# A gated delta-rule mixer: the last query-key projection of a chunk pair goes ahead of the fourth value projection

## What is computed

```python
q, k, v = x @ w_q, x @ w_k, x @ w_v
beta = sigmoid(x @ w_b) * 2.0
g = -exp(A_log) * softplus(x @ w_a + dt_bias)
q, k, v = [silu(causal_conv4(t, w)) for t, w in ((q, conv_q), (k, conv_k), (v, conv_v))]
q, k = l2norm(q), l2norm(k)                      # per head
for t in range(2048):                            # state S, 64 x 128 for each head
    S = S * exp(g[t])
    delta = (v[t] - k[t] @ S) * beta[t]
    S = S + outer(k[t], delta)
    o[t] = (q[t] * 64 ** -0.5) @ S
y = rms(o) * norm_w * silu(x @ w_g)
x = layernorm(x + y @ w_out)
```

## Time and profile before

| | |
|---|---|
| median of 3 runs | 5403.3 us (5380.4 to 5431.31) |
| profiled execution | 5445.98 us, of which 5444.2 us lie between its first and last instruction |
| mean granted TensorE clock | 0.882 |
| TensorE busy over the whole span | 4832.6 us, 89% |
| VectorE, ScalarE, GpSimd busy | 70%, 49%, 44% |
| query products of the first mixer (L467) | first at 110.5, last at 2623.5 us |
| two chunks, from one odd query product to the next | 160.9 us (1257.71 to 1418.60) |

### The profile page before, as it was taken

One profiled execution on the slowest core, in us unless ns is written; L12 is line 12 of the kernel. 1 busy time (PEld: TensorE's weight loads), 2 busy tenths in 40 slices (PEclk: granted clock), 3 DMA queues, 4 the chain that ended last, 5 costly groups with the idle time before them and its releaser, 6 DMA issues. The chain is left out here.

```text
span 5444.2 us, 111113 instructions
## 1 busy us (share of the span) xinstructions
PE 4832.6 (89%) x40474; PEld 3433.7 (63%) x40474; DVE 3796.7 (70%) x8919; ACT 2685.8 (49%) x6583; POOL 2375.8 (44%) x1924
## 2 busy tenths in 40 slices
PE   5999999999999999999889989984488778998998
PEld 3776777777777777777756556641166666664665
DVE  5666766777666766776488568746799657866874
ACT  2444444544444444454378568734300116865882
POOL 2434434445444544443367357414322116743751
PEclk6888988999898898998799899986699758998998
DMA  2000000000000000000100000000000000000000
GB/s 86 5 9 8 7 10 7 7 9 9 6 9 10 7 7 10 7 7 9 34 1 0 25 5 0 0 7 0 8 1 1 1 6 24 0 25 5 0 0 16
DMA packets 170107, 52.92 MB, mean 10 GB/s; under 512 B 142304, under 2 KB 166112, under 8 KB 168928
## 3 DMA queue, kind: packets, MB, share of 16 engines
q1 hardware_dynamic: 168160, 44.24, 3.7%
q10 hardware_dynamic: 1536, 3.21, 0.2%
HBM read 36.92 MB, written 10.49 MB: 9 GB/s over the span
## 5 line engine op out<-in xcount | busy, mean ns | idle before, releaser
L865 DVE SCALAR_TENSOR_TENSOR gd_qkT<-gd_ps,gd_w_qk,gd_qkT 128x256 f32<-128x256 f32 x768 | 367.4, 483 | 192.5 <-ACT gd_qkT L686 171.9
L430 PE MATMUL gd_ps<-gd_taps,gd_xwins 128*128 128x512 f32 x1024 | 464.6, 596 | 0.0
L1641 ACT ACTIVATE L_ffn_s<-L_ffn_s,L_ffn_nb,L_ffn_r 128x128 f32<-128x128 f32 x1024 | 419.5, 482 | 3.1
L1461 POOL TENSOR_TENSOR L_ffn_t<-L_ffn_t 128x512 f32<-128x512 f32 x128 | 190.2, 1486 | 394.5 <-DVE L_ffn_t L1682 394.5
L430 PEld LDWEIGHTS gd_ps<-gd_taps,gd_xwins 128*128 128x128 f32 x1024 | 192.4, 191 | 190.8 <-issue 185.2
L1079 POOL TENSOR_TENSOR gd_gV<-gd_g,cst 128x512 f32<-128x512 f32 x128 | 130.3, 1040 | 381.4 <-PE gd_ps L546 381.4
L1680 DVE TENSOR_TENSOR L_ffn_t<-L_ffn_ps,L_ffn_sb_rope 128x512 f32<-128x512 f32 x256 | 176.9, 691 | 101.6 <-PE L_ffn_ps L1486 101.6
L751 ACT ACTIVATE gd_X<-gd_o 128x128 f32<-128x128 f32 x512 | 150.4, 296 | 192.1 <-DVE gd_o L963 192.1
L1130 POOL TENSOR_TENSOR gd_gate<-gd_gate,gd_o 128x512 f32<-128x512 f32 x128 | 159.2, 1275 | 173.0 <-DVE gd_o L963 173.0
L1529 PEld LDWEIGHTS L_ffn_ps<-L_ffn_kT,L_ffn_qT 64*64 64x64 f32 (+1 forms) x4096 | 149.5, 137 | 114.3 <-issue 98.8
L1118 POOL TENSOR_TENSOR gd_gV<-gd_Tc,cst 128x1024 f32<-128x1024 f32 x32 | 60.6, 1893 | 359.3 <-DVE gd_Tc L938 359.3
(11 more groups left out here) (396 smaller groups left out, 14348.1 us busy)
## 6 DMA issues: line engine op xcount, KB each, us to landing
L_ffn_sb_rope<-in_rope SPq DMA_DIRECT2D x4, 2048.0 KB, 8.3
gd_tap_row<-in_L_attn_conv_v SPq DMA_DIRECT2D x2, 2048.0 KB, 15.8
gd_blocks<-gd_nA SPq DMA_DIRECT2D x256, 16.0 KB, 1.7
gd_Z<-gd_blocks SPq DMA_DIRECT2D x32, 128.0 KB, 2.0
gd_inverses<-gd_Z SPq DMA_DIRECT2D x32, 128.0 KB, 1.7
gd_Tc<-gd_inverses SPq DMA_DIRECT2D x256, 16.0 KB, 1.9
L_ffn_sb_wqkv<-in_L_ffn_wqkv SPq DMA_DIRECT2D x4, 768.0 KB, 9.3
out<-out_tok SPq DMA_DIRECT2D x8, 256.0 KB, 2.6
```

The source lines that it names most:

```text
L430: ins = pe.matmul(ps[4 + i % 2][:], xwin(j)[:, t:t + P], taps[:, t, 512 * i:512 * (i + 1)], start=(t == 0), stop=(t == TAPS - 1))
L865: ins = dve.scalar_tensor_tensor(produced(j, i), ps[6 + i % 2][:, P + t:P + t + WIDE], w_tap[:, at, t:t + 1], produced(j, i), ALU.mult, AL ...
L1461: pool.tensor_tensor(t1[b][:, K], t1[b][:, K], t2[b][:, K], ALU.add).then_inc(la.k_sum.sem, 1)
L1641: ins = act.activation(s[b][:, i, k], s[b][:, i, k], ACT.Exp, scale=r[b][:, h:h + 1], bias=nb[b][:, i, k:k + 1])
```

## The change

`produce(n + 2, j, 7)` goes from behind the fourth value projection to directly behind `produce(n + 2, j, 6)`. On ScalarE the first tap of piece 7 goes from behind `silu_v(n + 1, 3)` to between silu 5 and silu 6, and silu 7 goes from behind `silu_v` to directly behind silu 6. Both hold for the bodies that project at all (`more`), which are 30 of 32. No wait changes its value, and VectorE, GpSimd and SyncE keep their programs.

```diff
                     if follows:
                         if more:
                             produce(n + 2, j, 6, bp, cp)
+                            produce(n + 2, j, 7, bp, cp)
                         project_v(n + 1, j + 1, 3)
-                        if more:
-                            produce(n + 2, j, 7, bp, cp)
                         q_products(n + 1, (j + 1) % GROUP)
                     output(n, more)
...
                         if more:
                             first_tap(n + 2, j, 6)
                             silu(n + 2, j, 5)
+                            first_tap(n + 2, j, 7)
                             silu(n + 2, j, 6)
+                            silu(n + 2, j, 7)
                         silu_v(n + 1, 3)
-                        if more:
-                            first_tap(n + 2, j, 7)
-                            silu(n + 2, j, 7)
```

## The result

The change took 5373.91 us (median of 11 runs, 5353.98 to 5441.46), the kernel before 5436.73 in the same set (11 runs): a ratio of 0.990, 95% interval 0.9861 to 0.994. Two later sets were less kind to it: 0.9991 (0.9956 to 1.0026) and 0.9956 (0.9925 to 0.9986). What differs most is the kernel before in the first set: its medians in the other sets are 5406.53, 5405.86 and 5403.62 us, with 23 to 35 runs each, while the change lies at 5373.91, 5397.62 and 5382.68. The plain mean of the three ratios is 0.995, some 28 us, about half of the 49 that were forecast. The direction is right, and the size is within the 1% that a measurement can hardly tell from no change; the absolute time was forecast 20 to 44 us too low. The gain of the first set alone, 54 us by its ratio, is close to the forecast, but much of that is luck: the kernel before was slow in that set.

A forecast was written before the change was run, and what follows sets the result against it. TensorE was taken as the bound (95% busy in the first mixer), through its idle places and time at the lower clock. Gains of 21 + 15 + 5 + 8 = 49 us off the median 5403.3 gave 5354 us, range 5305 to 5410.

The forecast's parts named there:

- Odd chunks, the wait: Chunks whose query products read the pair just projected: silu 7 ends 1.42 us earlier, shortening TensorE's 3.05 us wait; 21 us.
- Odd chunks, the clock: Query products to output's end: with less idle ahead, the stretch returns from 6.98 us towards 5.83 at clock 1.00; 15 us.
- nearer to the even chunks: Odd chunks' remaining waits, 0.91 and 0.72 us, resemble even chunks' 0.61 us idle at clock 1.00; basis for 15 us.
- Even chunks, the solve's start: In the other chunks the inverses' DMA transfer and the solve come 0.35 us earlier, wait 1.37 to 0.72; 5 us.
- The GpSimd collision: Scaling of v and last square both fall into VectorE's inverse, 1.50 us blocked; one more loss of 0.75 than before.
- the prediction's second estimate: At the inverse: two GpSimd instructions back to back block VectorE 2.08 us, not 1.50, making the sum 41 us.
- The solves' clock: Even solves regain clock as their DMA wait shrinks, odd solves lose some; 8 us net, bounds 0 and 44.
- some of them will get a wait of their own: Odd solves are reached 1.42 + 1.0 us earlier, transfers only 0.35; new waits can eat most of 29 us regained.
- 26 us of idle time: Gain without clock: 21 us from the odd chunks' wait plus 5 us from the even chunks' solve start.
- The 23 us of clock: Gain from a higher TensorE clock: 15 us in the odd query-products-to-output stretch plus 8 us in the solves.
- rival 1: The clock gives nothing back, since remaining idle of 0.91 + 0.72 us lowers it: gain 26 us, 5377 us; chance 0.22.
- The sign that was named: If the mean clock of the mixer stays at 0.89, the forecast's clock terms are wrong.

The follow-up runs named there:

- fill: Kernel before plus three useless matmuls of 512 columns in front of the odd query products, timed in two sets: ratios 1.0065 and 1.0094 to before.
- act_only: Kernel before with only ScalarE's half of the change (first tap 7 and silu 7 earlier), TensorE in its old order: ratio 1.0069 to before.
- small_pool: The change with GpSimd's scaling of the fourth value piece and its last square cut to few columns, leaving work out: ratio 0.9959 to before.
- square_act: The change with the last square moved from GpSimd to ScalarE, behind the value silu: ratio 0.9951 to before.
- both: The change with ScalarE's first tap of piece 6 earlier and the last square on ScalarE: 5328.35 us, ratio 0.9875 to before.
- dve_late: The change with the first copy of VectorE's inverse done four times instead of once: median 5467.12 us, ratio 1.0122 to before.
- after_b: The change itself, unaltered, timed and profiled a third time beside the kernel before: 5382.68 us, ratio 0.9956.

## Why the prediction came out as it did

- **Odd chunks, the wait (21 us forecast): right.** From the end of the turning of y to the query products an odd chunk took 7.79 us before and 6.38 after, 1.41 less where 1.42 was forecast; 0.80 and 0.56 stand where 0.91 and 0.72 were worked out.
- **Odd chunks, the clock (15): right in its place.** The stretch fell from 6.98 and 6.67 in the two profiles of before to 5.82 in all three of the change, 13 to 17 us. fill shows the cause, the idle time ahead, and also that such a gain need not reach the whole. act_only adds that the loss does not grow evenly with the idle time, as "nearer to the even chunks" assumes: 2.57 us of it left 14 of 15 stretches at clock 1.00.
- **Even chunks, the solve's start (5): about right.** The DMA wait fell to 0.78, 0.73 and 0.72 (0.72 forecast). With the 1.07 that the new wait and the drained projection cost ahead of the value projection, and the 0.69 that the stretch to the output won, an even chunk starts its solve 0.2 us earlier, 3 us in 15. The GpSimd collision was sized at 2 x 0.75. The two rows of 1.00 and 0.97 take 2.01 from start to end, where two undisturbed ones take some 0.43 (0.21 each): 1.58 lost, so the prediction's second estimate, 2 x 1.04 = 2.08, was too large. Each of the two VectorE instructions began 0.09 and 0.13 us after a GpSimd instruction and ended 0.05 and 0.06 us after that one's end, so it was held until then, and lost at most what was left of the 1.04. The Trainium skill, SBUF — State Buffer, section "Who interferes with whom", says that a VectorE instruction with two SBUF inputs contends with a GpSimd instruction that reads SBUF, and that the lock is exclusive. The trace agrees with that. small_pool shows that the collision is what the even solves waited for.
- **The solves' clock (8, bounds 0 and 44): the step that failed in its reason.** Even solves: 23.55 us as the mean of two profiles before, 22.28 as the mean of three after, 19 us won in 15. Odd solves: 20.32 and 21.28, 14 us lost, though the two profiles of before differ by as much (20.79 and 19.85). Net 5 us, close to the 8, and that is luck, for it is not because "some of them will get a wait of their own": the waits before odd solves went on average only from 0.42 to between 0.48 and 0.55, and in small_pool and square_act, without any such wait, they are slower still. The prediction took each solve's clock to hang on the wait in front of it. Over the kernels the even solves roughly follow that wait (21.1 to 21.7 us at 0.43 to 0.45, 22.1 to 22.5 at 0.64 to 0.78, 23.4 to 23.9 at 1.3 to 1.5, 27.8 at 2.13 in act_only; dve_late, whose profiled execution was far above its median, is out of line, 25.9 at 1.32). But even and odd together are 43 to 44.5 us in all profiles but those of both (41.6), act_only (46.2) and dve_late (49.6): where one kind was faster, the other was mostly slower. That the one causes the other is not shown, and what sets an odd solve's clock stays open.
- **The sum.** 26 us of idle time were forecast, and 26 to 28 came at equal clock, in three sets. The 23 us of clock came in neither of the two sets where the clock of the kernel before is listed: 20 us were lost in the one (0.8874 against 0.8914) and 10 in the other (0.8902 against 0.8922). In the first set the whole ratio was 0.990; the clock of the kernel before is not listed there, and a median of 5436.73 would by the line be one of about 0.885. So the outcome is near the sum of rival 1 (5377), though not by its mechanism: the clock does come back in the stretch that was named, but the whole execution shows no such gain. Where it went is not located: the profiles show none lost in the 15 pairs of chunks, and the rest of the execution varies by more. The sign that was named, a mixer clock that stays at 0.89, did not decide either: the 15 pairs ran at 0.90 to 0.91 with the change, and at 0.89 and 0.91 before.
- **What misled.** The profile of before was one execution at 0.882, and 49 us were taken off the median as if all of it were the kernel's. In a kernel with a varying clock the terms of idle time repeat to a few us; the terms of the clock, read from one execution, do not.

## What to carry to other kernels

Take the idle terms and the clock terms of a forecast apart, and believe the first: for ten kernels the waits and stretches in the profile gave the time at equal clock within 8 us, while the clock regained in one stretch did not show in the time of the whole. Compare timed runs by time and mean granted clock together, for two kernels can change places through the clock alone. And when a wait is removed in front of an engine, look at once for what its cause then meets: here two GpSimd instructions slid into the inverse, and moving one of them to ScalarE, with an earlier tap for VectorE, took 44 us off at equal clock in place of 26, and with its higher clock made the whole gain more than twice as large.

## What the runs showed of the hardware

- The same instructions take different times in different executions: the part from the last odd query products to the end, whose code no kernel here changes, took 2872.83 us in after_b and 2906.51 in fill_b, at clocks of 0.89 and 0.88, with VectorE's busy time the same to 1.2 us. The two profiles of before alone differ there by 20 us (2899.28 and 2879.56). The windows of after_b and fill_b:

```profile
2499.77:5372.60 2872.83, 2431.80 (x18310) 1587.16 (x18310) 2065.64 (x4195) 1525.92 (x3228) 1258.35 (x951) 0.89 0.03 8
```

```profile
2528.49:5435.00 2906.51, 2466.67 (x18310) 1617.68 (x18310) 2064.48 (x4195) 1524.87 (x3227) 1257.72 (x950) 0.88 0.02 8
```

- Keeping TensorE busy did not keep its clock up over the whole: 2.6 us of work of no use (3.05 less 0.47) in each of 15 places brought the stretch behind them to 1.00 and left the mean clock 0.007 to 0.009 lower, in two sets.
- Odd solves with the same 0.42 us in front of them ran now wholly at 2.4 GHz, now for much of their length at 1.2 GHz, 17.7 (at clock 1.00) to 23.8 us for the same work; one of the longest, from the first profile of before, at 0.68:

```profile
1438.08:1461.90 23.82, 23.33 (x352) 19.78 (x352) 12.88 (x42) 12.47 (x36) 4.56 (x5) 0.68 0.01 3
```

- A VectorE instruction of 0.2 us that met a GpSimd instruction of 1.04 us took 0.95 to 1.00 us and ended some 0.05 us after it, in the kernel before as in the change.
